# Delta times u plus one: multiplied by VectorE, turned once, copied by ScalarE

## The chip, the cores and the metric

The kernel runs on one core of one Trainium2 chip. The metric is the device time of one launch in microseconds. The kernel before takes 713.55 us (median of 3 runs, 712.55 to 714.0).

## What is computed

A transformer block on 4 sequences of 1024 tokens with 128 channels: a modulated layer norm, a selective state scan as the mixer, a second norm, and a mixture of 8 experts of which each token takes 2. The part that the change touches is the input of the scan:

```python
def _selective_scan(u, A_log, x_proj_w, dt_proj_w, dt_proj_b, D_skip):
    xp = u @ x_proj_w
    delta = jax.nn.softplus(xp[..., :DT_RANK] @ dt_proj_w + dt_proj_b)
    Bm = xp[..., DT_RANK:DT_RANK + N_STATE]
    Cm = xp[..., DT_RANK + N_STATE:]
    A = -jnp.exp(A_log)
    dA = jnp.exp(delta[..., None] * A)
    dBu = delta[..., None] * Bm[:, :, None, :] * u[..., None]
    def step(h, inp):
        dA_t, dBu_t, C_t = inp
        h = dA_t * h + dBu_t
        y = jnp.einsum('bdn,bn->bd', h, C_t)
        return (h, y)
```

u has 256 channels and comes out of a sigmoid. The kernel keeps it as the tanh of half its argument, so that the true value is half of "u plus one"; hence the factor (u + 1) in the code. There are 16 states n.

## The kernel before, in words

The 4096 tokens are cut into 8 segments f of 512 tokens. Channels lie on the 128 partitions, in two halves a. The main loop runs over 128 steps k = 16 s + n: window s works on segment s, step n on state n. In a step, ScalarE makes dA = exp(A delta) for both halves (`decay`, L1013) and scales part of duT, which is delta times (u + 1) with tokens on the partitions, by the token's B (`scale_in`, L1005); GpSimd scales the rest of it (L542). TensorE turns the scaled blocks S back to channels on the partitions (`turn_in`), VectorE scans 512 tokens (`scan`, L1367) into a ring of 6 slots, GpSimd multiplies the ring by C (L559), and TensorE adds it up (`add_state`). Each engine's order is fixed by hand: the instructions stand in program order and every cross-engine dependence is a semaphore.

Everything else is put into "gaps": a step has two, gap 2n and 2n+1, after its first and its second half. `gap_work` calls, in each engine's program, `front` (norm, u, gate of a coming segment), `project` (xproj, delta, B, and duT of the next segment, f = s + 1) and `tail` and `routing` of segments before. Two windows numbered -2 and -1 stand ahead of the loop and hold the gap work of the first segments alone; I call them the prologue. After the last window come 71 expert tiles and 8 sums, the tile stage.

Buffers tie the engines together: S has 3 slots, the banks of turned blocks are 3, dA has 6 slots (3 steps). So ScalarE can be about two steps ahead of VectorE, no more. GpSimd makes its part of S two steps ahead. PSUM banks FA (`front`) and FB (`project`) are each used by one piece after the other, so TensorE waits until the piece before has been read.

In the kernel before, u of each half is turned into FA (gaps 30 and 1, `turns("uT..")`), and VectorE adds one while it copies it to `uT` (L1096, gaps 31 and 2). The later gate product uses FA too and waits for that read. Delta (L1124, gaps 20 and 23) is turned into FB at gaps 24 and 26, and VectorE multiplies it by `uT` into `duT` (L1109, gaps 25 and 27). `scale_in` of the next window's first step, which ScalarE reaches right after gap 27, waits for the second of these.

Of the kernel before, what the change touches and what calls it, by code (L numbers as in the profile page):

```python
# [7 lines left out]
ALU = mybir.AluOpType  # L8
# [4 lines left out]
P = 128  # L13
# [66 lines left out]
def adaln_kernel(nc, xT_d, w1_d, w2_d, wo_d, xproj_d, dtw_d, alog_d, conv_d, cols_d, bo_d, router_d,  # L80
# [5 lines left out]
    with ctx:  # L86
# [63 lines left out]
        gate = sb("gate", [P, 3, HALVES, BANK])  # L150
        uT = sb("uT", [P, CS, MLP])
        duT = sb("duT", [P, 2, CS, MLP])
# [47 lines left out]

        front_all = uT[:, :, :].rearrange("p c m -> p (c m)")
        xs, xsT = tiles_of(front_all, 0, XS_SLOTS, ROW), tiles_of(front_all, (XS_SLOTS + 1) * P, 2)
# [41 lines left out]
        def PO(k):  # L244
            return bank((5, 0)[k % 2])[:, 0:P]

        PIECES = ["raw", "xn", "u0", "u1", "gate0", "gate1", "uT0", "uT1",
                  "xproj", "bt", "dt0", "dt1", "dT0", "dT1",
# [14 lines left out]
        tlog, tseed, tstep, trs_ready = (sem(n) for n in ("tlog", "tseed", "tstep", "trs_ready"))  # L263
        staged = [sem(f"staged{k}") for k in range(2)]
        av_ready, e_ready, lw_ready, w_ready, softplus_step, delta_ready = (
            sem(n) for n in ("av_ready", "e_ready", "lw_ready", "w_ready", "softplus_step", "delta_ready"))
# [319 lines left out]
        def _(pe):  # L586
# [39 lines left out]
            def front(gap, f):  # L626
# [19 lines left out]
                if gap == 0:  # L646
                    product(FB[0:PROJ, :], xproj[:, 1, :], u[:, f % 2, 1, :], False, True).then_inc(filled["xproj"], 1)
                    last_read["FB"] = (read["xproj"], f + 1)
                if gap in (30, 1):
                    a = int(gap == 1)  # L650
                    turns(f"uT{a}", "FA", f + 1, u[:, f % 2, a, :])

            def project(gap, f):
# [12 lines left out]
                if gap in (24, 26):  # L666
                    a = (gap - 24) // 2
                    turns(f"dT{a}", "FB", f + 1, delta[:, f % 2, a, :])

# [217 lines left out]
        def _(act):  # L887
# [39 lines left out]
            def project(gap, f):  # L927
# [10 lines left out]
                if gap in (9, 10):  # L938
                    a = gap - 9
                    act.wait_ge(av_ready, f * HALVES + a + 1)  # L940
                    nc.scalar.activation(ev[:, a, :], ev[:, a, :], ACT.Exp, scale=-1.0).then_inc(e_ready, 1)  # L941
                if gap == 18:
                    act.wait_ge(e_ready, (f + 1) * HALVES)
                    nc.scalar.activation(lw[:, :, :], ev[:, :, :], ACT.Ln, bias=1.0).then_inc(lw_ready, 1)  # L944
# [138 lines left out]
        def _(dve):  # L1083
# [7 lines left out]

            def front(gap, f):
                if gap in (31, 2):
                    a = int(gap == 2)
                    dve.wait_ge(filled[f"uT{a}"], f + 1)
                    V.tensor_scalar(uT[:, :, a * P:(a + 1) * P], FA.rearrange("p (c d) -> p c d", c=CS), 1.0, None, ALU.add  # L1096
                                    ).then_inc(read[f"uT{a}"], 1)

            def project(gap, f):
                if gap in (19, 20, 22, 23):  # L1100
                    softplus((gap - 19) // 3, (gap - 19) % 3, f)
                if gap in (25, 27):
                    a = (gap - 25) // 2
                    dve.wait_ge(filled[f"dT{a}"], f + 1)
                    dve.wait_ge(read[f"uT{a}"], f + 1)
                    if f > 1:
                        dve.wait_ge(scaled_act, act_scaled((f - 1) * NSTATE - 1))
                        dve.wait_ge(scaled_pool, pool_scaled((f - 1) * NSTATE - 1))
                    V.tensor_tensor(duT[:, f % 2, :, a * P:(a + 1) * P], uT[:, :, a * P:(a + 1) * P],  # L1109
                                    FB.rearrange("p (c d) -> p c d", c=CS), ALU.mult).then_inc(read[f"dT{a}"], 1)  # L1110

# [228 lines left out]
            def gap_work(gap, window):  # L1340
# [12 lines left out]
                if inner_ is not None:  # L1353
                    project(gap, inner_)
                if front_ is not None:
                    front(gap, front_)

# [191 lines left out]
```

## Time and profile before

| what | value |
|---|---|
| median of the runs | 713.55 us (712.55 to 714.0) |
| profiled execution | 714.06 us, span 712.3 us |
| PE (TensorE) busy | 622.1 us, 87% |
| DVE (VectorE) busy | 552.2 us, 78% |
| ACT (ScalarE) busy | 545.1 us, 77% |
| POOL (GpSimd) busy | 512.0 us, 72% |
| chain that ended last | PE 43%, ACT 38%, DVE 9%, issue 6%, DMA 2% |

The span is the time from the first to the last instruction of one profiled execution. The shares of busy time are averages over three stages: the prologue to 56 us, the scan windows to about 510 us, and the tile stage, in which TensorE is nearly always busy. The windows of the middle stage are the part to read.

### The profile page before, as it was taken

Reading aid. Unit: us, or ns where it says so; the run is one execution under the profiler, and the core shown is the slowest. Engines: PE = TensorE matmul, PEld = TensorE weight load, DVE = VectorE, ACT = ScalarE, POOL = GpSimd, SP = SyncE. Lnnn points to the kernel's source line nnn. Section 1 sums busy time; section 2 is a strip of 40 time slices with the busy share of each in tenths; the row PEclk is TensorE's granted clock in tenths of the full one; section 3 lists DMA queues with packets and bytes.
Section 4 is the critical chain, followed back from the end, with each engine's and each line's share of the span. In section 5 each row is a group of like instructions: output and inputs, shape, how many; then the busy total and the mean of one; then the engine's idle time right before and its main releaser. Section 6 shows DMA issues by size and latency. Waiting matters only on the chain.

```text
span 712.3 us, 14511 instructions
## 1 busy us (share of the span) xinstructions
PE 622.1 (87%) x4435; PEld 518.5 (73%) x4435; DVE 552.2 (78%) x1170; ACT 545.1 (77%) x1024; POOL 512.0 (72%) x479
## 2 busy tenths in 40 slices
PE   3897789989989988988997997878768999999995
PEld 3444767857767766775775776767667899999994
DVE  4347779899898989989989999889944486555553
ACT  3268989988997997997999799798817656656550
POOL 3147969878899799989989989968915457644441
PEclk9989999999999999999999999979979999999997
DMA  7030436345834554444533563393501122222535
GB/s 232 0 121 2 132 86 163 103 121 159 255 103 111 160 138 107 112 127 125 146 96 107 128 162 103 103 239 119 133 17 51 56 65 84 83 67 63 169 124 186
DMA packets 65196, 82.93 MB, mean 116 GB/s; under 512 B 6960, under 2 KB 55152, under 8 KB 61024
## 3 DMA queue, kind: packets, MB, share of 16 engines
q1 hardware_dynamic: 59648, 70.78, 36.6%
q0 software_dynamic: 4320, 9.12, 3.8%
q10 hardware_dynamic: 1152, 2.10, 0.8%
q8 instruction: 38, 0.62, 0.4%
q14 instruction: 38, 0.31, 0.1%
HBM read 52.19 MB, written 29.78 MB: 115 GB/s over the span
## 4 chain that ended last, share of the span: by engine, by line
PE 43%; ACT 38%; DVE 9%; issue 6%; DMA 2%; POOL 0%; DVEq 0%; ACTq 0%; SPq 0%; POOLq 0%
PE psum L588 28%; PE psum L592 15%; ACT S L1005 14%; ACT dA L1013 13%; DVE ring L1367 4%; ACT xn L909 1%; ACT L1013 1%; ACT L944 1%; DMA ring<-results 1%; ACT soft L937 1%; ACT soft L936 1%; ACT soft L944 1%; ACT hT L891 1%; ACT soft L941 1%; ACT u L914 1%
## 5 line engine op out<-in xcount | busy, mean ns | idle before, releaser
L559 POOL TENSOR_TENSOR ring<-ring,Cb 128x1024 f32<-128x1024 f32 x128 | 279.5, 2185 | 37.0 <-DVE ring L1367 36.4
L592 PEld LDWEIGHTS psum<-ident,S 128*128 128x128 f32 x1024 | 119.4, 143 | 115.0 <-issue 66.8
L592 PE MATMUL psum<-ident,S 128*128 128x128 f32 x1024 | 159.7, 280 | 45.2 <-POOL S L542 12.1
L1013 ACT ACTIVATE dA<-delta,A 128x512 f32<-128x512 f32 x256 | 178.8, 717 | 10.2 <-DVE ring L1367 10.2
L1005 ACT ACTIVATE S<-duT,BT 128x256 f32<-128x256 f32 x384 | 166.6, 502 | 24.5 <-DVE duT L1109 21.2
L592 PE MATMUL psum<-ident,ring 128*128 128x128 f32 x1088 | 159.6, 278 | 4.7 <-DMA ring<-results 4.6
L1367 DVE TENSOR_TENSOR_SCAN ring<-dA,state,psum 128x512 f32<-128x512 f32 x128 | 157.8, 1264 | 1.3 <-PE psum L592 0.6
L1367 DVE TENSOR_TENSOR_SCAN ring<-dA,psum 128x512 f32<-128x512 f32 x128 | 150.4, 1206 | 10.4 <-PE psum L592 10.1
L592 PEld LDWEIGHTS psum<-ident,ring 128*128 128x128 f32 x1088 | 129.5, 144 | 5.8 <-DMA ring<-results 5.2
L580 POOL DMA_INDIRECT results<-xn,result_at x71 | 69.1, 974 | 85.7 <-DVE xn L1496 79.0
L588 PE MATMUL psum<-uT,S 128*128 128x128 f32 x852 | 110.3, 281 | 3.8 <-DVE uT L1478 3.3
L588 PEld LDWEIGHTS psum<-uT,S 128*128 128x128 f32 x852 | 104.3, 197 | 4.8 <-issue 4.8
L1062 ACT COPY S<-gateup_w 128x736 f32 x71 | 57.0, 805 | 51.4 <-PE psum L588 49.9
L542 POOL TENSOR_TENSOR S<-duT,BT 128x256 f32<-128x256 f32 x112 | 75.7, 677 | 5.9 <-DVE duT L1109 5.0
L1501 DVE TENSOR_TENSOR S<-S,psum 128x384 f32<-128x384 f32 x71 | 39.2, 552 | 50.2 <-ACT S L1072 46.5
L472 POOL DMA_INDIRECT token_rows<-h2r,pos x64 | 65.0, 1016 | 17.8 <-issue 9.6
L588 PE MATMUL psum<-hT,w1c 128*128 128x512 f32 x128 | 67.6, 629 | 2.1 <-ACT hT L891 2.1
L588 PE MATMUL psum<-soft,S 128*128 (+1 forms) x426 | 59.5, 276 | 2.0 <-DVE S L1501 1.9
L588 PEld LDWEIGHTS psum<-soft,S 128*128 128x128 f32 (+1 forms) x426 | 53.2, 192 | 2.8 <-issue 2.8
L1072 ACT ACTIVATE S<-psum 128x384 f32<-128x384 f32 x71 | 34.8, 490 | 25.0 <-PE psum L588 24.3
L508 POOL TENSOR_SCALAR xT<-xT,gabo 128x1024 f32<-128x1024 f32 x4 | 11.5, 2870 | 33.5 <-PE psum L592 25.0
L1478 DVE COPY uT<-psum 128x128 f32<-128x128 f32 x71 | 20.5, 289 | 13.9 <-PE psum L592 13.7
(226 smaller groups left out, 745.1 us busy)
## 6 DMA issues: line engine op xcount, KB each, us to landing
Cb<-c_rows SPq DMA_DIRECT2D x32, 1024.0 KB, 6.0
token_rows<-zeros SPq DMA_DIRECT2D x64, 272.0 KB, 7.1
uT<-token_rows SPq DMA_DIRECT2D x71, 68.0 KB, 1.8
ring<-results SPq DMA_DIRECT2D x8, 512.0 KB, 5.0
xT<-in_xT SPq DMA_DIRECT2D x4, 512.0 KB, 5.1
out_T<-xT ACTq DMA_DIRECT2D x8, 256.0 KB, 2.3
stage<-in_xT SPq DMA_DIRECT2D x6, 256.0 KB, 7.3
gateup_w<-in_gate SPq DMA_DIRECT2D x1, 1408.0 KB, 10.2
```

What stands on the lines that cost most here:

```text
L472: nc.gpsimd.indirect_dma_start(token_rows, bass.IndirectOffsetOnAxis(ap=pos[:, j, g * CS + c:g * CS + c + 1], axis=0), h2r[:, j, g * CS + ...
L542: nc.gpsimd.tensor_tensor(S[:, k % S_SLOTS, CS - own:, :], duT[:, s % 2, CS - own:, :], BT[:, s % 2, CS - own:, n:n + 1].to_broadcast([P, ...
L559: nc.gpsimd.tensor_tensor(ring[:, k % RING, :, 0:BANK], ring[:, k % RING, :, 1:], Cb[:, group_ % 2, own, :].unsqueeze(1).to_broadcast([P, ...
L580: nc.gpsimd.indirect_dma_start(results, bass.IndirectOffsetOnAxis(ap=result_at[:, t % (2 * XS_SLOTS):t % (2 * XS_SLOTS) + 1], axis=0), ob[ ...
L588: return nc.tensor.matmul(out, lhsT, rhs, start=start, stop=stop)
L592: return nc.tensor.matmul(out, block_in, ident[at, at], is_transpose=True, start=start, stop=True, skip_group_check=True)
L1005: nc.scalar.activation(S[:, k % S_SLOTS, c, :], duT[:, s % 2, c, :], ACT.Identity, scale=BT[:, s % 2, c, n:n + 1]).then_inc(scaled_act, 1)
L1013: nc.scalar.activation(dA[:, (k * HALVES + a) % DA_SLOTS, :], delta[:, s % 2, a, :], ACT.Exp, scale=A[:, a, n:n + 1]).then_inc(da_ready, 1)
L1062: nc.scalar.copy(both_w[:, par % 2, :], gateup_w[:, ds(e * 2 * INTER, INTER + NIN * P)]).then_inc(weights_copied, 1)
L1072: nc.scalar.activation(silu[:, par % 2, :], PG(par)[:, 0:NIN * P], ACT.Silu).then_inc(silu_ready, 1)
L1367: V.tensor_tensor_scan(ring[:, k % RING, a, 1:], dA[:, (k * HALVES + a) % DA_SLOTS, :], db(k, a), state[:, n, a:a + 1] if s % SEG else 0.0 ...
L1501: V.tensor_tensor(innerT[:, par % 2, :], silu[:, par % 2, :], PU(par)[:, 0:NIN * P], ALU.mult).then_inc(inner_ready, 1)
```

## The change

The sum and the product change places. VectorE multiplies (u + 1) by delta with channels on the partitions into a new buffer `du` in one instruction per half, after delta (gaps 21 and 24). TensorE turns `du` in the places in which it turned delta (gaps 24 and 26). ScalarE copies the turned block from FB to `duT` (gaps 25 and 27). The turning of u, its copy and the multiplication of turned blocks are gone. `du` takes the memory of `uT`. Both tensors that the new product reads lie in SBUF; each of the removed instructions read one from PSUM.

```diff
@@ tensor engine
-                if gap in (30, 1):
-                    a = int(gap == 1)
-                    turns(f"uT{a}", "FA", f + 1, u[:, f % 2, a, :])
@@
                 if gap in (24, 26):
                     a = (gap - 24) // 2
-                    turns(f"dT{a}", "FB", f + 1, delta[:, f % 2, a, :])
+                    pe.wait_ge(du_ready, HALVES * f + a + 1)
+                    turns(f"dT{a}", "FB", f + 1, du[:, a, :])
@@ scalar engine
+                if gap in (25, 27):
+                    a = (gap - 25) // 2
+                    act.wait_ge(filled[f"dT{a}"], f + 1)
+                    if f > 1:
+                        act.wait_ge(scaled_pool, pool_scaled((f - 1) * NSTATE - 1))
+                    nc.scalar.copy(duT[:, f % 2, :, a * P:(a + 1) * P], FB.rearrange("p (c d) -> p c d", c=CS)
+                                   ).then_inc(read[f"dT{a}"], 1)
@@ vector engine
-            def front(gap, f):
-                if gap in (31, 2):
-                    a = int(gap == 2)
-                    dve.wait_ge(filled[f"uT{a}"], f + 1)
-                    V.tensor_scalar(uT[:, :, a * P:(a + 1) * P], FA.rearrange("p (c d) -> p c d", c=CS), 1.0, None, ALU.add
-                                    ).then_inc(read[f"uT{a}"], 1)
@@
-                if gap in (25, 27):
-                    a = (gap - 25) // 2
-                    dve.wait_ge(filled[f"dT{a}"], f + 1)
-                    dve.wait_ge(read[f"uT{a}"], f + 1)
-                    if f > 1:
-                        dve.wait_ge(scaled_act, act_scaled((f - 1) * NSTATE - 1))
-                        dve.wait_ge(scaled_pool, pool_scaled((f - 1) * NSTATE - 1))
-                    V.tensor_tensor(duT[:, f % 2, :, a * P:(a + 1) * P], uT[:, :, a * P:(a + 1) * P],
-                                    FB.rearrange("p (c d) -> p c d", c=CS), ALU.mult).then_inc(read[f"dT{a}"], 1)
+                if gap in (21, 24):
+                    a = (gap - 21) // 3
+                    dve.wait_ge(delta_ready, HALVES * f + a + 1)
+                    dve.wait_ge(read[f"u{a}"], f + 1)
+                    wait(dve, filled[f"dT{a}"], f)
+                    V.scalar_tensor_tensor(du[:, a, :], u[:, f % 2, a, :], 1.0, delta[:, f % 2, a, :], ALU.add, ALU.mult
+                                           ).then_inc(du_ready, 1)
```

VectorE, window 2 from the second scan of step 10 to the scans of step 12 and on, in the kernel before (L1117 to L1124 make delta, L1089 is the norm before the router, the scans are L1367):

```order
L1367 SCALAR_TENSOR_TENSOR ring<-dA,psum 128x512 x2
L1117 SCALAR_TENSOR_TENSOR soft<-psum,soft 128x512
L1118 SCALAR_TENSOR_TENSOR psum<-psum,soft 128x512
L1367 SCALAR_TENSOR_TENSOR ring<-dA,psum 128x512
L1089 TENSOR_SCALAR xn<-psum,tstat,trs 128x128 x4
L1121 TENSOR_TENSOR psum<-soft,psum 128x512
L1124 TENSOR_TENSOR delta<-soft,psum 128x512
L1367 SCALAR_TENSOR_TENSOR ring<-dA,psum 128x512 x2
L1109 TENSOR_TENSOR duT<-uT,psum 128x4x128
L1367 SCALAR_TENSOR_TENSOR ring<-dA,psum 128x512 x2
L1109 TENSOR_TENSOR duT<-uT,psum 128x4x128
```

The same place in the changed kernel (its lines: scan L1362, delta L1114 to L1121, norm L1095, the new product L1106):

```order
L1362 SCALAR_TENSOR_TENSOR ring<-dA,psum 128x512
L1106 SCALAR_TENSOR_TENSOR du<-u,delta 128x512
L1362 SCALAR_TENSOR_TENSOR ring<-dA,psum 128x512
L1114 SCALAR_TENSOR_TENSOR soft<-psum,soft 128x512
L1115 SCALAR_TENSOR_TENSOR psum<-psum,soft 128x512
L1362 SCALAR_TENSOR_TENSOR ring<-dA,psum 128x512
L1095 TENSOR_SCALAR xn<-psum,tstat,trs 128x128 x4
L1118 TENSOR_TENSOR psum<-soft,psum 128x512
L1121 TENSOR_TENSOR delta<-soft,psum 128x512
L1362 SCALAR_TENSOR_TENSOR ring<-dA,psum 128x512
L1106 SCALAR_TENSOR_TENSOR du<-u,delta 128x512
L1362 SCALAR_TENSOR_TENSOR ring<-dA,psum 128x512 x6
```

The two products moved ahead: the first now stands before the first scan of step 11, the second between the two scans of step 12, and no gap work stands between the scans of steps 12 to 14.

ScalarE, the same stage of window 2, before (L1005 is the scaling, L1013 the decay, L891 the second norm's modulation):

```order
L1013 ACTIVATE dA<-delta,A 128x512 x2
L1005 ACTIVATE S<-duT,BT 128x256 x3
L1013 ACTIVATE dA<-delta,A 128x512
L891 ACTIVATE hT<-psum,mod 128x512
L1013 ACTIVATE dA<-delta,A 128x512
L1005 ACTIVATE S<-duT,BT 128x256 x3
L1013 ACTIVATE dA<-delta,A 128x512
```

And after (scaling L1011, decay L1019, modulation L890, the new copy L946):

```order
L1019 ACTIVATE dA<-delta,A 128x512 x2
L946 COPY duT<-psum 128x4x128
L1011 ACTIVATE S<-duT,BT 128x256 x3
L1019 ACTIVATE dA<-delta,A 128x512
L890 ACTIVATE hT<-psum,mod 128x512
L1019 ACTIVATE dA<-delta,A 128x512
L946 COPY duT<-psum 128x4x128
L1011 ACTIVATE S<-duT,BT 128x256 x3
```

The first copy stands ahead of the scaling for step 15, the second ahead of the scaling for the next window's first step.

## Rows read from the trace of the kernel before

**Rows 1.** Busy time by engine in one scan window; columns: stretch, length, busy (instructions):

```profile
200.57:259.53 58.96, 53.41 (x375) 42.27 (x374) 53.99 (x82) 54.63 (x109) 53.55 (x50) 1.00 0.48 125
```

**Rows 2.** Waits by engine and line; columns: total us, times, longest:

```profile
ACT S L1005 <- DVE duT L1109: 21.2, 7, 3.7
```

**Rows 3.** Chain of waits, 200 to 260 us; columns: start, length, what:

```profile
214.26 1.94 PE psum L592 x16
...
225.32 0.20 DVE stat L1164
```

**Rows 4.** Groups of instructions by line; columns: count, busy us, mean ns, idle before:

```profile
L1096 DVE TENSOR_SCALAR uT<-psum 128x512 f32<-128x512 f32 x16 | 10.9, 683 | 5.3 <-PE psum L592 5.1
L1109 DVE TENSOR_TENSOR duT<-uT,psum 128x512 f32<-128x512 f32 x16 | 10.8, 675 | 5.6 <-PE psum L592 5.4
L1117 DVE SCALAR_TENSOR_TENSOR soft<-psum,soft 128x512 f32<-128x512 f32 x16 | 10.8, 674 | 5.5 <-ACT soft L944 4.7 <-ACT psum L949 0.8
L914 ACT ACTIVATE u<-psum,zhalf 128x512 f32<-128x512 f32 x16 | 10.8, 678 | 12.3 <-PE psum L621 9.5 <-PE psum L588 2.7
L1437 DVE TENSOR_TENSOR w1c<-ring 128x1024 f32<-128x1024 f32 x1 | 2.0, 1974 | 0.0
```

**Rows 5.** Timeline of window 2's end and window 3's start; columns: start, length, what [idle before]:

```profile
220.91 1.31 ACT L1005 ACTIVATE S<-duT,BT 128x256 f32<-128x256 f32 x3 [3.72 <-DVE duT L1109]
...
226.78 0.66 DVE L1096 TENSOR_SCALAR uT<-psum 128x512 f32<-128x512 f32 x1
...
232.27 0.69 DVE L1096 TENSOR_SCALAR uT<-psum 128x512 f32<-128x512 f32 x1
...
245.51 2.20 POOL L559 TENSOR_TENSOR ring<-ring,Cb 128x1024 f32<-128x1024 f32 x1 [0.63 <-DVE ring L1367]
```

**Rows 6.** Timeline of window 3, steps 10 to 15, three engines:

```profile
266.01 2.44 DVE L1367 TENSOR_TENSOR_SCAN ring<-dA,state,psum 128x512 f32<-128x512 f32 x2
267.15 0.22 POOL L492 TENSOR_SCALAR trs<-tstat 128x4 f32<-128x4 f32 x1
269.16 0.63 PE L592 MATMUL psum<-ident,S 128*128 128x128 f32 x4 [1.74 <-POOL S L542]
273.05 2.19 POOL L559 TENSOR_TENSOR ring<-ring,Cb 128x1024 f32<-128x1024 f32 x1
273.32 2.44 DVE L1367 TENSOR_TENSOR_SCAN ring<-dA,state,psum 128x512 f32<-128x512 f32 x2
275.19 0.61 POOL L542 TENSOR_TENSOR S<-duT,BT 128x256 f32<-128x256 f32 x1
277.58 0.60 PE L592 MATMUL psum<-ident,S 128*128 128x128 f32 x4
279.22 0.62 POOL L542 TENSOR_TENSOR S<-duT,BT 128x256 f32<-128x256 f32 x1
281.06 0.60 PE L592 MATMUL psum<-ident,S 128*128 128x128 f32 x4
```

**Rows 7.** Timeline of VectorE beside GpSimd where the tile stage starts:

```profile
514.52 4.30 POOL L559 TENSOR_TENSOR ring<-ring,Cb 128x1024 f32<-128x1024 f32 x2
...
518.01 0.84 DVE L1484 TENSOR_TENSOR result_at<-uT,aside 128x1 int32<-128x1 f32 x1
```

**Rows 8.** The line L1484 by itself; columns: duration ns min/median/max:

```profile
L1484 DVE TENSOR_TENSOR result_at<-uT,aside x71: 146/149/843, 518.0 to 690.0; 128x1 int32<-128x1 f32 x71
```

**Rows 9.** Timeline of the prologue:

```profile
32.32 1.88 PE L588 MATMUL psum<-u,xproj 128*96 128x512 f32 x4
35.42 1.13 PE L588 MATMUL psum<-hT,w 128*128 128x512 f32 x2 [0.78 <-DVE uT L1096]
56.03 1.31 ACT L1005 ACTIVATE S<-duT,BT 128x256 f32<-128x256 f32 x3 [1.97 <-DVE duT L1109]
```

**Rows 10.** Timeline of window 0, end:

```profile
92.72 0.69 DVE L1117 SCALAR_TENSOR_TENSOR soft<-psum,soft 128x512 f32<-128x512 f32 x1 [4.11 <-ACT soft L944]
108.03 1.31 ACT L1005 ACTIVATE S<-duT,BT 128x256 f32<-128x256 f32 x3 [2.73 <-DVE duT L1109]
```

More of the change, by code:

```diff
@@ L150, in adaln_kernel @@
         gate = sb("gate", [P, 3, HALVES, BANK])
-        uT = sb("uT", [P, CS, MLP])
+        du = sb("du", [P, HALVES, BANK])
         duT = sb("duT", [P, 2, CS, MLP])
@@ L199, in tiles_of @@
             return area[:, at:at + count * width].rearrange("p (k h) -> p k h", k=count)
-        front_all = uT[:, :, :].rearrange("p c m -> p (c m)")
+        front_all = du[:, :, :].rearrange("p a t -> p (a t)")
         xs, xsT = tiles_of(front_all, 0, XS_SLOTS, ROW), tiles_of(front_all, (XS_SLOTS + 1) * P, 2)
@@ L245, in PO @@
             return bank((5, 0)[k % 2])[:, 0:P]
-        PIECES = ["raw", "xn", "u0", "u1", "gate0", "gate1", "uT0", "uT1",
+        PIECES = ["raw", "xn", "u0", "u1", "gate0", "gate1",
                   "xproj", "bt", "dt0", "dt1", "dT0", "dT1",
@@ L264, in adaln_kernel @@
         staged = [sem(f"staged{k}") for k in range(2)]
+        du_ready = sem("du_ready")
         av_ready, e_ready, lw_ready, w_ready, softplus_step, delta_ready = (
@@ L1354, in gap_work @@
                     project(gap, inner_)
-                if front_ is not None:
-                    front(gap, front_)
             def scan(k, a):
```

## The prediction

> **What bounds the kernel now.** I read the table of stretches first, then the waits, the chain, and at last the timelines of single windows, engine beside engine. A full window takes 58.96 us, and in it four engines are busy 53.4, 54.0, 54.6 and 53.6 us [rows 1]: no engine is the bound alone, and each has only some 5 us to spare. ScalarE's longest wait is for the multiplication into duT: 21.2 us in 7 waits, one at each window's end, 3.7 us at most [rows 2]. That looks like the prize of this change, and I think that it is not. The question is what holds the window while ScalarE waits.
>
> Going through one period: TensorE takes up work at 214.26 and is on the chain until VectorE gets the router's logits at 225.32 [rows 3]. The next window shows who had released it: TensorE waits 1.74 us at 269.16 for GpSimd's part of S [rows 6]; at 214.26 I take it for the same. Further ahead, at 245.51, GpSimd itself waited for VectorE's scan [rows 5]. So a period is: VectorE from the logits (225.3) to the scan that GpSimd waits for (245.5), some 20 us; GpSimd from there to its S just ahead of the product at 273.05 [rows 6], 28 us; TensorE for the rest of the 58.96, some 11 us, to the next logits. ScalarE is ahead of all this by its two steps of buffers, and its 3.7 us are slack.
>
> **The change part by part.** The sum is made against the profiled execution (714.06 us, span 712.3); I carry the difference over to the median, 713.55.
>
> 1. Removed in the VectorE part of the period. The two additions of one cost 0.683 us each [rows 4], and both lie at 226.78 and 232.27, in the 20 us where VectorE paces [rows 5]. I count 0.6 of each, since the records of neighbours overlap a little: 1.2 us a boundary. Five boundaries have them beside the routing work (segments 3 to 7): -6.0 us if all else follows.
>
> 2. Removed on TensorE: 16 groups of four turns of u, 0.60 us each by the record of a like group (277.58 [rows 6]), and a wait of the gate product for VectorE. In the windows they lie behind the logits, where VectorE paces, and I give them nothing.
>
> 3. ScalarE's copies, 16. The nearest row is its reading of a 128x512 bank, 0.678 us [rows 4], some 0.57 behind another. Both stand between the scaling for step 14 and that for the next window's first step, where ScalarE waits 3.72 us now [rows 5]. The first makes it wait in its own queue for the first turned half; behind it stand the scaling of step 15 and two decays, each needed some microseconds later by scans that are not yet due. The second can start when the second turned half is there, which is where VectorE's multiplication started before, and takes the same time. So the handoff gains nothing but about 0.1 us, and the copies cost nothing while the 3.7 us are there. Without that cover they would cost 2 x 0.57 = 1.15 us a window.
>
> 4. VectorE's new products, 16. Duration between 0.674, the like instruction with one tensor in PSUM, and 0.99, half of the one large instruction that reads SBUF alone, which took 1.974 for twice the elements [rows 4]. I take 0.68; that one had a strided operand. They take the place of multiplications of 0.675, so VectorE's work in this part is as before, but it stands before the second scan of step 12, which TensorE needs: that scan ends at 275.7, and TensorE's turn of step 14's S comes at 277.58 [rows 6], a slack of 1.8 us, of which 1.2 go for the two products.
>
> 5. What the new products meet. The L1484 at 518.01, which reads two SBUF tensors, took 0.84 us where the median of its 71 is 0.149 [rows 8]; it ended at 518.85, and GpSimd's products ended at 518.82 [rows 7]. All the other instructions of VectorE in the scan windows have an operand in PSUM and run beside GpSimd without loss. So a new product may have to wait for GpSimd's present instruction: between 0 and 2.19 us (the ring product at 273.05 [rows 6]), 16 times; and GpSimd may have to wait for it in turn, 0 to 0.68 us. The page "SBUF — State Buffer" of the Trainium skill (section "SBUF: two separate sides") says just that: a VectorE instruction with two SBUF inputs and a GpSimd instruction that reads SBUF exclude each other for the whole instruction, whichever starts first; by that rule, the trace agrees for the one direction that it shows.
>
> The phase decides the size. The first product comes after the second scan of step 10, at about 267.2, where GpSimd has small instructions of 0.2 us (267.15) [rows 6]: VectorE gets in at once, and GpSimd, which paces here, is put back by up to 0.6. The second comes after step 12's first scan, at about 274.5; GpSimd's ring product runs from 273.05 to 275.2 and its S from 275.19 to 275.8 [rows 6]. With GpSimd 0.6 earlier than now, VectorE meets the end of the one or the whole of the other: 0.1 to 0.7 us. If it waits for the S as well, the scan is late, GpSimd's S for step 15 (279.22) is late, and TensorE, which takes it at 281.06 [rows 6], loses what was left. So of 1.2 us gained a boundary, 0.6 goes to the first product and 0 to 0.6 to the second: I take -0.3 a boundary, 5 x -0.3 = -1.5 us.
>
> 6. Windows 0 and 1 have no routing, and are paced by ScalarE's logarithm, then VectorE from 92.72 to the duT at 108.03, then ScalarE again [rows 10]. The products (+1.2) and the turn of step 14 with the copy behind it come in place of two multiplications; with what the second product waits for S I get between -0.2 and +0.5 for each: +0.3 for both.
>
> 7. The prologue. The xproj product starts a turn (0.5) earlier, and the gate product, which started at 35.42, follows it at its end, 34.20 [rows 9]: -1.7. At the other end the tanh of the next segment, done in the wait before 56.03 till now, comes behind the copies: +0.5. So -1.2.
>
> The tile stage is as it was. Sum: -1.5 + 0.3 - 1.2 = **-2.4 us**, 711.7 for the profiled execution, 711.2 for the median.
>
> **The rivals.**
> - Only the prologue gains, the windows give nothing: 713.55 - 1.2 = 712.4. For it: half of point 5's range. Chance 0.15.
> - No mutual waiting of note: point 1 in full, the additions gone and nothing lost, 5 x -1.2, with -1.7 from the prologue: 705.9. Against it: rows 7. Chance 0.16.
> - Slower, by VectorE caught behind whole ring products. Place: the second product before step 12's second scan, and the first one in windows 0 and 1, where GpSimd waits for the same scan. Price: 2.2 us for a product caught, less the slack of 1.8 - 1.2 = 0.6; with the first product's 0.6 on GpSimd and -1.2 from point 1 some +1.0 a window for five, +1.5 for each of the first two, -1.2 for the prologue: +6.8, 720.3. It decides from about 1.2 us of waiting a window on. Chance 0.14.
> - Slower, by ScalarE becoming the bound: then 7 x 1.15 less the prologue's gain, +6.9: 720.4. Against it: it would be busy 54.6 + 1.15 = 55.8 of 58.9. Chance 0.05.
> - The wait of rows 2 was the real limit: 21.2 less 14 copies of 0.57, less the prologue: 713.55 - 13.2 - 1.2 = 699.1. Against it: rows 3 and 6, where TensorE and GpSimd work without a pause while ScalarE waits. Chance 0.05.
>
> **How the numbers follow.** My forecast has 0.45, its own range 708.5 to 714. A run can tell 0.2% from no change, 1.4 us. Faster by more: 0.36 of my 0.45, 0.16 and 0.05, with a little of the first rival, 0.58. Within: 0.20. Slower: 0.14 + 0.05 and 0.03 from mine, 0.22. The range 705.5 to 717 leaves out the last rival and half of the two slow ones.
>
> **What the profile after would show.** Right: products on VectorE with a mean above 0.68 us and some of 0.8 to 1.3; the small GpSimd instructions or the S beside them late; ScalarE's wait at the window's end for the turned half instead of duT, still 1 to 3 us; windows of 58.3 to 58.9 us; the first S at about 54.8. Wrong: products of 2 us and more (then slower), products all at 0.68 and windows near 57.7 (then the second rival), or a ScalarE without waits.

## The result, and the profile after

The changed kernel takes 715.78 us (median; 713.81 to 718.69), the kernel before on the same chip 714.01 (711.94 to 715.58): ratio 1.0024, 95% interval 1.0014 to 1.0034. The forecast was 711.2; the time moved the other way, by 1.8 us. The profiled span is 714.2 us for 712.3.

The stretches of two windows in the changed kernel (columns as in [rows 1]):

```profile
201.38:261.28 59.90, 53.40 (x374) 42.05 (x375) 54.86 (x83) 55.75 (x111) 55.22 (x50) 1.00 0.47 127
261.28:320.77 59.49, 51.72 (x361) 40.42 (x360) 53.29 (x82) 55.64 (x111) 53.82 (x50) 1.00 0.45 123
```

The window that took 58.96 us [rows 1] takes 59.90. ScalarE has its copies more (55.75 for 54.63 us). GpSimd is busy 1.7 us longer with the same 50 instructions: something holds them. The waits of ScalarE and GpSimd in the whole changed kernel (total us, times, longest):

```profile
ACT duT L946 <- PE psum L593: 23.8, 15, 4.2
POOL ring L560 <- DVE ring L1362: 37.1, 33, 5.5
```

ScalarE's wait of [rows 2] is gone by name and is back before its copies, as large as it was (23.8 for 21.2 us): that fits slack, and e4 below shows that it is. GpSimd's wait for scans is hardly larger in sum than before (37.1 for 36.4 us), but it has moved, as the timelines show. The groups that answer to [rows 4] (count, busy us, mean ns, idle before):

```profile
L1106 DVE SCALAR_TENSOR_TENSOR du<-u,delta 128x512 f32<-128x512 f32 x16 | 13.9, 867 | 0.1
L1114 DVE SCALAR_TENSOR_TENSOR soft<-psum,soft 128x512 f32<-128x512 f32 x16 | 10.8, 678 | 6.8 <-ACT soft L950 6.6
L946 ACT COPY duT<-psum 128x512 f32<-128x512 f32 x16 | 9.4, 586 | 23.8 <-PE psum L593 23.8
```

The product has a mean of 0.867 us; its like with one operand in PSUM keeps 0.678. Which of them are long shows in the timeline of window 3, steps 10 to 15, the place of [rows 6]:

```profile
267.06 0.20 POOL L497 TENSOR_TENSOR trs<-trs 128x4 f32<-128x4 f32 x1
267.26 0.67 DVE L1106 SCALAR_TENSOR_TENSOR du<-u,delta 128x512 f32<-128x512 f32 x1
267.34 0.64 POOL L499 TENSOR_SCALAR trs<-trs 128x4 f32<-128x4 f32 x1
...
273.99 1.27 DVE L1362 TENSOR_TENSOR_SCAN ring<-dA,state,psum 128x512 f32<-128x512 f32 x1
274.97 0.61 POOL L543 TENSOR_TENSOR S<-duT,BT 128x256 f32<-128x256 f32 x1
275.18 0.95 DVE L1106 SCALAR_TENSOR_TENSOR du<-u,delta 128x512 f32<-128x512 f32 x1
276.06 5.96 DVE L1362 TENSOR_TENSOR_SCAN ring<-dA,state,psum 128x512 f32<-128x512 f32 x5
277.41 2.19 POOL L560 TENSOR_TENSOR ring<-ring,Cb 128x1024 f32<-128x1024 f32 x1 [1.83 <-DVE ring L1362]
280.79 0.62 POOL L543 TENSOR_TENSOR S<-duT,BT 128x256 f32<-128x256 f32 x1
281.51 0.63 PE L593 MATMUL psum<-ident,S 128*128 128x128 f32 x4 [0.36 <-issue]
```

The first product gets in at once and GpSimd's 0.20 us instruction takes 0.64. The second runs into GpSimd's S and takes 0.95, ending 0.55 after that S. Then comes a wait that the prediction did not have: GpSimd, its S done, waits 1.83 us for the second scan of step 12, which stands behind the second product. In the kernel before the same place reads

```profile
275.84 2.19 POOL L559 TENSOR_TENSOR ring<-ring,Cb 128x1024 f32<-128x1024 f32 x1
```

without a wait: that scan ended at 275.76 [rows 6], 0.08 us ahead. Where GpSimd did wait, in the changed kernel, it starts 0.08 us after the scan too, so there was no slack at all. By window, from 0 to 6, GpSimd started 0.08, 0.08, 0.78, 0.08, 0.70, 0.08 and 1.44 us after this scan in the kernel before, and 0.08 in each in the changed one. In windows 2 to 6 the second product took 1.43, 0.95, 1.27, 0.95 and 1.90 us; in windows 0 and 1, and as the first product everywhere, 0.66 to 0.69. The long ones of windows 2, 4 and 6 met the tail of a ring product and not only an S. In window 2:

```profile
213.67 2.18 POOL L560 TENSOR_TENSOR ring<-ring,Cb 128x1024 f32<-128x1024 f32 x1
214.99 1.43 DVE L1106 SCALAR_TENSOR_TENSOR du<-u,delta 128x512 f32<-128x512 f32 x1
215.82 1.06 POOL L543 TENSOR_TENSOR S<-duT,BT 128x256 f32<-128x256 f32 x1
217.62 2.19 POOL L560 TENSOR_TENSOR ring<-ring,Cb 128x1024 f32<-128x1024 f32 x1 [0.74 <-DVE ring L1362]
```

The product ends at 216.41, 0.56 after the ring product's end, GpSimd's S has 1.06 us instead of 0.61, and GpSimd waits 0.74 for the scan. So windows 2 and 4 show a wait of 0.74 and a held S, windows 3 and 5 a wait of 1.83.

For the prologue, [rows 9]: the first scaling starts 1.28 us earlier.

```profile
54.75 1.30 ACT L1011 ACTIVATE S<-duT,BT 128x256 f32<-128x256 f32 x3
```

What follows is measured by one mark a window, VectorE's first reading of the router's logits, whose start the trace gives to 0.01 us. There are eight marks, in windows 1 to 7 and one in the tile stage; the four periods from window 1's to window 5's are compared, in one profiled execution of each kernel. Before it stands at 166.30 (window 1) and at 401.43 (window 5): four windows take 235.13 us. After: 165.87 and 403.46, 237.59 us, +0.62 a window. The same stretch of every other kernel (e15 and e16 repeat two of them, and show how far one profile is to be trusted: e15 differs from after by 0.30 a window, almost all of it in one period, e16 from e5 by 0.01):

| kernel | four windows | a window, against before | median us | ratio (95%) |
|---|---|---|---|---|
| before | 235.13 | | 713.5 to 714.4 | 1 |
| after | 237.59 | +0.62 | 715.78 | 1.0024 (1.0014 to 1.0034) |
| after again (e15) | 238.82 | +0.92 | 715.19 | 1.0020 (1.0005 to 1.0034) |
| products behind delta (e1) | 240.84 | +1.43 | 721.85 | 1.0106 (1.0089 to 1.0124) |
| the same, PSUM operand (e2) | 236.62 | +0.37 | 717.64 | 1.0049 (1.0033 to 1.0065) |
| without u (e3) | 232.04 | -0.77 | 708.59 | 0.9928 (0.9910 to 0.9945) |
| before with ScalarE's copies (e4) | 235.11 | 0.00 | 714.46 | 1.0008 (0.9993 to 1.0022) |
| after, PSUM operand (e5) | 235.62 | +0.12 | 714.21 | 1.0010 (0.9998 to 1.0022) |
| the same again (e16) | 235.56 | +0.11 | 713.07 | 0.9988 (0.9973 to 1.0002) |
| after without products (e6) | 231.89 | -0.81 | 706.25 | 0.9911 (0.9888 to 0.9934) |
| copies by VectorE (e7) | 238.16 | +0.76 | 716.58 | 1.0055 (1.0034 to 1.0076) |
| u plus one by ScalarE (e8) | 234.98 | -0.04 | 715.38 | 1.0030 (1.0017 to 1.0044) |
| first product alone (e9) | 234.01 | -0.28 | 710.01 | 0.9933 (0.9913 to 0.9953) |
| second product alone (e10) | 235.47 | +0.09 | 712.26 | 0.9968 (0.9957 to 0.9979) |
| additions at gaps 9 and 11 (e11) | 237.78 | +0.66 | 716.35 | 1.0042 (1.0024 to 1.0059) |
| products at gaps 24 and 26 (e12) | 241.10 | +1.49 | 722.55 | 1.0123 (1.0101 to 1.0145) |
| lock-free behind the scan (e13) | 231.90 | -0.81 | 708.29 | 0.9913 (0.9893 to 0.9932) |
| segment 0 alone (e14) | 235.12 | 0.00 | 710.16 | 0.9944 (0.9924 to 0.9965) |

The median has a second part that the windows do not explain. In the session of e15, nine executions of the changed kernel had a mean granted clock of 0.957 to 0.967 and took 713.9 to 718.3 us, three had 0.974 to 0.976 and took 713.9 to 715.3; the kernel before had 0.970 to 0.978 and took 711.7 to 715.8. Why the changed kernel has the lower clock more often, and how much of the 1.8 us goes with it, was not tested. The arguments below therefore rest on the marks first.

### The profile page after: what moved, and what is told of

The parts are those of the page before. It is cut to its first block and busy times, and to the rows that moved or that the text cites. A ratio compares the mean times of both kernels' runs of the same rounds, so it can differ in the third digit from the quotient of the medians.

```text
span 714.2 us, 14394 instructions
## 1 busy us (share of the span) xinstructions
PE 613.6 (86%) x4371; PEld 510.1 (71%) x4371; DVE 548.0 (77%) x1154; ACT 554.2 (78%) x1040; POOL 516.6 (72%) x479
## 5 line engine op out<-in xcount | busy, mean ns | idle before, releaser
L560 POOL TENSOR_TENSOR ring<-ring,Cb 128x1024 f32<-128x1024 f32 x128 | 280.4, 2192 | 37.6 <-DVE ring L1362 37.1
L1019 ACT ACTIVATE dA<-delta,A 128x512 f32<-128x512 f32 x256 | 178.5, 715 | 4.9 <-DVE ring L1362 4.7
L1011 ACT ACTIVATE S<-duT,BT 128x256 f32<-128x256 f32 x384 | 166.6, 502 | 0.6
L1362 DVE TENSOR_TENSOR_SCAN ring<-dA,psum 128x512 f32<-128x512 f32 x128 | 150.7, 1207 | 17.1 <-PE psum L593 15.5
L1362 DVE TENSOR_TENSOR_SCAN ring<-dA,state,psum 128x512 f32<-128x512 f32 x128 | 158.4, 1267 | 4.4 <-PE psum L593 2.8
L589 PE MATMUL psum<-du,S 128*128 128x128 f32 x852 | 110.9, 282 | 3.8 <-DVE du L1473 3.3
L589 PEld LDWEIGHTS psum<-du,S 128*128 128x128 f32 x852 | 104.5, 198 | 4.8 <-issue 4.8
L543 POOL TENSOR_TENSOR S<-duT,BT 128x256 f32<-128x256 f32 x112 | 77.3, 691 | 6.1 <-ACT duT L946 5.1
L589 PE MATMUL psum<-hT,w1c 128*128 128x512 f32 x128 | 66.1, 616 | 2.1 <-ACT hT L890 2.1
L593 PE MATMUL psum<-ident,du 128*128 128x128 f32 x135 | 30.0, 282 | 6.0 <-DVE delta L1121 3.5
```

The lines of the kernel that those rows point to most:

```text
L543: nc.gpsimd.tensor_tensor(S[:, k % S_SLOTS, CS - own:, :], duT[:, s % 2, CS - own:, :], BT[:, s % 2, CS - own:, n:n + 1].to_broadcast([P, ...
L560: nc.gpsimd.tensor_tensor(ring[:, k % RING, :, 0:BANK], ring[:, k % RING, :, 1:], Cb[:, group_ % 2, own, :].unsqueeze(1).to_broadcast([P, ...
L589: return nc.tensor.matmul(out, lhsT, rhs, start=start, stop=stop)
L593: return nc.tensor.matmul(out, block_in, ident[at, at], is_transpose=True, start=start, stop=True, skip_group_check=True)
L1011: nc.scalar.activation(S[:, k % S_SLOTS, c, :], duT[:, s % 2, c, :], ACT.Identity, scale=BT[:, s % 2, c, n:n + 1]).then_inc(scaled_act, 1)
L1019: nc.scalar.activation(dA[:, (k * HALVES + a) % DA_SLOTS, :], delta[:, s % 2, a, :], ACT.Exp, scale=A[:, a, n:n + 1]).then_inc(da_ready, 1)
```

## The experiments

Theory A: VectorE's product with two SBUF inputs and GpSimd shut each other out, and the windows lose by it. Theory B: ScalarE's two copies make the windows longer.

**e1 and e2: the exclusion by itself.** Both put the products directly behind delta; they differ in one operand. Both also have TensorE's first turn wait for both products, and ScalarE's next write to FB for the first, so the pair is clean between its two kernels and not against the kernel before.

```diff
-                if gap in (21, 24):
+                if gap in (20, 23):
...
-  V.scalar_tensor_tensor(du[:, a, :], u[:, f % 2, a, :], 1.0, delta[:, f % 2, a, :], ALU.add, ALU.mult)
+  V.scalar_tensor_tensor(du[:, a, :], u[:, f % 2, a, :], 1.0, FB, ALU.add, ALU.mult)      # e2 only
```

> The changed kernel with each product of VectorE standing directly behind the delta that it multiplies (gaps 20 and 23 instead of 21 and 24); ScalarE's next write to FB waits for the first product, TensorE's first turn for both. The pair to the next kernel, which differs only in where the second operand lies. Theory A (VectorE's product with two SBUF inputs and GpSimd shut each other out, and the windows lose by it): products of 0.67 to 2 us, mean over 0.75; time 712 to 718 us, and 2 to 5 us above the next kernel. Theory B (the windows are longer because ScalarE now has two copies more): as long as the next kernel, within 1 us.

> As the kernel before it, but the product reads FB (in PSUM) in place of delta, so its value lacks the masked logarithm: one SBUF and one PSUM input, same order, same count. Theory A: all 16 products at 0.67 to 0.70 us, GpSimd's small instructions at 0.2, time 709 to 713 us. Theory B: same time as its pair within 1 us, near 715.

The product's group in e1, then in e2:

```profile
L1106 DVE SCALAR_TENSOR_TENSOR du<-u,delta 128x512 f32<-128x512 f32 x16 | 16.8, 1050 | 0.6
```

```profile
L1106 DVE SCALAR_TENSOR_TENSOR du<-u,psum 128x512 f32<-128x512 f32 x16 | 11.0, 687 | 0.6
```

4.2 us between the pair, 1.06 a window: the exclusion is real and costs, and Theory B, which had them alike, falls here. But both came out 4 to 5 us above what Theory A expected of them. Without any exclusion e2 is still slower than before. So something beside the exclusion costs, the place of the products or those waits (TensorE waits 1.1 us for the products in each of windows 2 to 5 of e1, 0.8 to 0.9 in two of them in e2).

**e3: the removal alone.**

```diff
-  if gap in (30, 1): turns(f"uT{a}", "FA", f + 1, u[:, f % 2, a, :])
-  V.tensor_scalar(uT[...], FA..., 1.0, None, ALU.add)
-  V.tensor_tensor(duT[...], uT[...], FB..., ALU.mult)
+  V.tensor_scalar(duT[...], FB..., 1.5, None, ALU.mult)
```

> The kernel before without the turns of u and the additions of one (TensorE's and VectorE's), and with the multiplication by the turned u replaced by one by a constant (so u is left out of duT): what the removal alone brings. By the prediction's points 1 and 7: 7 to 8 us less than before, 706. By the trace of the changed kernel, where the stage of 20 us behind the logits got only 0.3 us shorter instead of 1.2: 1 to 3 us less, 711 to 713, of which 1.2 in the prologue.

708.6 us lies between the two ranges: 5.5 us less, 0.77 a window for the 1.2 of the prediction. Why not 1.2 shows behind the logits in e6, which has the same removal. TensorE, let through earlier by VectorE, waits 1.16 us for the S of step 66 (window 4, step 2):

```profile
282.73 1.30 ACT L1010 ACTIVATE S<-duT,BT 128x256 f32<-128x256 f32 x3
286.68 0.62 POOL L543 TENSOR_TENSOR S<-duT,BT 128x256 f32<-128x256 f32 x1
287.40 0.63 PE L593 MATMUL psum<-ident,S 128*128 128x128 f32 x4 [1.16 <-ACT S L1010]
```

The profile puts this wait down to ScalarE, but the rows counted by step say otherwise: ScalarE's part of that S was done at 284.03, GpSimd's at 287.30, 0.10 us before TensorE starts. In the kernel before the same turn, at 290.59, waited 0.40 us, again until 0.10 after GpSimd's part. So it is with all 80 waits of over 0.3 us for an S between window 1's mark and window 5's in before, after, e3 and e6: they end 0.10 us after GpSimd's part and 2.9 us or more after ScalarE's. GpSimd is the one that TensorE waits for, and the page's chain, which gives ScalarE 38% in the kernel before, goes wrong at such places.

In the kernel before, GpSimd waits for scans only in the first third of these periods. Behind window 2's, in the kernel before, it waits 0.81, 1.39 and 0.63 us; in e6 the first of these is gone, the others are 1.38 and 0.63. The place of the first, before and then in e6:

```profile
237.99 2.19 POOL L559 TENSOR_TENSOR ring<-ring,Cb 128x1024 f32<-128x1024 f32 x1 [0.81 <-DVE ring L1367]
```

```profile
234.68 2.17 POOL L560 TENSOR_TENSOR ring<-ring,Cb 128x1024 f32<-128x1024 f32 x1
```

That is 12.67 us after the mark (225.32) and 11.84 after it (222.84): 0.83 us gained, as much as GpSimd had waited there and not the whole of VectorE's 1.2.

**e4: ScalarE's copies alone.**

```diff
+                if gap in (25, 27):
+                    act.wait_ge(filled[f"dT{a}"], f + 1)
+                    nc.scalar.copy(ev[:, a, :], delta[:, f % 2, a, :])
```

> The kernel before with ScalarE's two extra copies of 128x512 a window in the places of the changed kernel (gaps 25 and 27, each waiting for the turned half as there), from delta to a free buffer; nothing else changed. Theory A: 0 to 1 us slower than before, 714 to 715. Theory B: 3 to 6 us slower, 717 to 720, with ScalarE's wait at the window's end gone and its scaling late for TensorE.

1.0008, and 0.00 us a window: the copies cost nothing, as the prediction had it. In its profile the period from window 5's mark to window 6's is 60.02 us for 57.76, outside the four that are compared; its median does not show that, and the cause stays open.

**e5: the changed kernel with a PSUM operand, every place kept.**

```diff
+                    k, half = (f - 1) * NSTATE + 11 + a, a
+                    dve.wait_ge(turned_in, k * HALVES + half + 1)
-  ... delta[:, f % 2, a, :], ALU.add, ALU.mult)
+  ... db(k, half), ALU.add, ALU.mult)
```

> The changed kernel, every instruction in its place, but the product of segments 1 to 7 reads in place of delta the PSUM bank that the next scan reads (after the same wait as that scan), so du has a wrong second factor: one SBUF and one PSUM input at the places of the change. What the mutual exclusion costs there. From the pair that was run (4.2 us with the products behind delta): all 14 products at 0.67 to 0.69 us, 711 to 713.5 us. If not the exclusion but the two places lose the time: 714.5 to 716.

All 14 at 0.66 us (mean 661 ns), but 714.2 us, above the 711 to 713.5 of the exclusion as the sole cause and just below the 714.5 to 716 of the places alone; per window 0.49 us less than after. Both take part. And with no exclusion left, GpSimd still waits for that scan:

```profile
274.23 0.62 POOL L543 TENSOR_TENSOR S<-duT,BT 128x256 f32<-128x256 f32 x1
274.89 0.66 DVE L1111 SCALAR_TENSOR_TENSOR du<-u,psum 128x512 f32<-128x512 f32 x1
...
275.47 5.96 DVE L1367 TENSOR_TENSOR_SCAN ring<-dA,state,psum 128x512 f32<-128x512 f32 x5
276.83 2.19 POOL L560 TENSOR_TENSOR ring<-ring,Cb 128x1024 f32<-128x1024 f32 x1 [1.98 <-DVE ring L1367]
```

This made the third theory: the product costs by its place, ahead of a scan that GpSimd takes up with no slack.

**e6 and e7: no products; copies by VectorE.**

```diff
-                    V.scalar_tensor_tensor(du[:, a, :], ...)                        # e6
-                    turns(f"dT{a}", "FB", f + 1, du[:, a, :])
+                    turns(f"dT{a}", "FB", f + 1, delta[:, f % 2, a, :])
...
-                    nc.scalar.copy(duT[...], FB...)                                 # e7
+                    V.tensor_copy(duT[...], FB...)
```

> The changed kernel without VectorE's products: TensorE turns delta as before, ScalarE copies it (u is left out of duT). If the products (0.67 us each, the waiting included) are what ate the gain of the removed additions: 706 to 708.5 us, near the kernel before without u. If ScalarE's copies ahead of its scaling ate it: 713 to 716.

> The changed kernel with the two copies a window made by VectorE in the places of the old multiplications (gaps 25 and 27) instead of ScalarE. If ScalarE's copies cost nothing, 1.35 us more on VectorE a window, of which half to all shows: 719 to 723 us. If ScalarE was the one that the change overloaded: 711 to 714.

Without products the whole gain of the removal is there: 0.9911, 0.81 a window. GpSimd's place reads

```profile
271.83 0.60 POOL L543 TENSOR_TENSOR S<-duT,BT 128x256 f32<-128x256 f32 x1
272.66 2.19 POOL L560 TENSOR_TENSOR ring<-ring,Cb 128x1024 f32<-128x1024 f32 x1 [0.23 <-DVE ring L1354]
```

0.23 us of waiting instead of 1.8 to 2.0. From e6 to e5 is the price of the lock-free products where the change has them: (235.62 - 231.89) / 4 = 0.93 us a window, for 1.32 us of work. TensorE's turns of du are not what costs: in windows 2 to 5 of e5 and of after it has no wait of over 0.4 us for a product. e3 (VectorE multiplies at gaps 25 and 27) and e6 (ScalarE copies there) have the same windows, to 0.04 us: behind the scan, VectorE's 1.35 us were free. e7 missed its expectation of 719 to 723: its copies at gaps 25 and 27 cost 0.14 a window against after, which is less than after and e15 differ, and 0.3% in the median, since that place is nearly free.

**e8: the removal by another way.**

```diff
-  turns of u at gaps 30 and 1, V.tensor_scalar(uT[...], FA..., 1.0, None, ALU.add) at gaps 31 and 2
+  turns of u at gaps 29 and 31, nc.scalar.activation(uT[...], FA..., ACT.Identity, bias=1.0) at gaps 31 and 1
```

> The kernel before, its multiplication of turned blocks kept, but u plus one copied out of FA by ScalarE (gaps 31 and 1) instead of VectorE (31 and 2), with TensorE's turns of u at gaps 29 and 31 instead of 30 and 1. It removes the same 16 VectorE instructions from the same stage as the change, adds as much to ScalarE, and brings no product with two SBUF inputs. If the removal is worth what the kernel without u showed (5.5 us) and ScalarE's work is nearly free (0.4 us for two copies a window): 708.5 to 711 us. If ScalarE's work behind the logits, or TensorE's turns in other places, cost more: 712 to 715.

The second case, and a little past it: nothing gained in the windows, 0.3% slower in all. Its edit does two things, ScalarE's added work and TensorE's turns in other places, and which of them eats the 0.77 us was not separated.

**e9 and e10: one product each.**

```diff
-                if gap in (21, 24):
+                if gap == 21:      # e9; e10: gap == 24
```

> The changed kernel with its first product alone (gap 21); the second half of delta is turned and copied without u. Without products it took 706.3 us, with both 715.8. Theory (the products stand ahead of step 12's second scan, for which GpSimd waits, so that each one's time shows there, and the second also meets GpSimd's S): the first costs 0.45 to 0.7 us a window and little in the prologue: 709 to 711.5 us, the smaller part. Rival (the loss is a matter of the second product and its mutual exclusion alone): 706 to 708 us.

> The changed kernel with its second product alone (gap 24); the first half of delta is turned and copied without u. Theory: 710.5 to 713 us, the larger part, its durations 0.67 to 1.5 us. Rival (the two places count alike and the exclusion is shared): the same as with the first alone within 1 us, near 711.

As the theory of the place had it, against e6: the first costs (234.01 - 231.89) / 4 = 0.53 us a window, the second (235.47 - 231.89) / 4 = 0.89, together 1.42, and with both (after) it is (237.59 - 231.89) / 4 = 1.42. GpSimd's ring product of step 12 in e9, then in e10:

```profile
274.51 2.18 POOL L560 TENSOR_TENSOR ring<-ring,Cb 128x1024 f32<-128x1024 f32 x1 [0.37 <-DVE ring L1363]
```

```profile
274.22 2.20 POOL L560 TENSOR_TENSOR ring<-ring,Cb 128x1024 f32<-128x1024 f32 x1 [1.82 <-DVE ring L1363]
```

The first product has VectorE and GpSimd late together; the second makes GpSimd wait. These rows are of window 3. By the profile of e15 instead of after, both together are 1.73 a window, so that the sum agrees to 0.3 us and no better.

**e11 and e12: other places.**

```diff
-  turns of u at gaps 30 and 1, additions at 31 and 2, raw rows turned at gap 10      # e11
+  turns of u at gaps 8 and 10, additions at 9 and 11, raw rows turned at gap 12
...
-  products at gaps 21 and 24, turns of du at 24 and 26, copies at 25 and 27          # e12
+  products at gaps 24 and 26, turns of du at 25 and 27, copies at 26 and 27
```

> The kernel before with the same turns of u and the same additions of one on VectorE, but moved out of the stretch behind the logits: turned at gaps 8 and 10 (the first window at 8 and 9), added at 9 and 11; TensorE's turn of the raw rows goes from gap 10 to 12. If VectorE's time is dear only behind the logits, where it paces, and about free from the scans of steps 4 and 5 on: 708.5 to 711 us. If it is as dear there (GpSimd waits for those scans), or TensorE's new waits for VectorE in FA cost what is gained: 713 to 716 us.

> The changed kernel with its products moved behind the place that was found dear: at gaps 24 and 26 instead of 21 and 24, turned at gaps 25 and 27, copied at 26 and 27. The first now stands where the second did, the second behind the first scan of step 13. If time ahead of step 12's second scan is dear and time behind it free: 0.7 us a window less ahead of it, 710.5 to 713 us, below the changed kernel. If the later handoff of duT makes ScalarE's scaling for the next window's first step late (it had 1.9 to 2.5 us of slack at the first copy), or the second product is held by GpSimd again: 714 to 719 us.

Both came out above even the slower of their two ranges, e11 by 0.4 us and e12 by 3.6. In e11 each window is 0.66 us longer than before, and VectorE's wait for ScalarE's logarithm is 11.4 us in sum for 4.7 before; whether the scans behind the additions or TensorE's turn of u in FA is to blame was not separated. e12 shows the exclusion at its dearest. Its second product starts 1.0 us into a ring product for whose scan GpSimd had waited, and has to sit out the rest:

```profile
281.67 2.19 POOL L560 TENSOR_TENSOR ring<-ring,Cb 128x1024 f32<-128x1024 f32 x1 [0.80 <-DVE ring L1362]
282.69 1.72 DVE L1106 SCALAR_TENSOR_TENSOR du<-u,delta 128x512 f32<-128x512 f32 x1
284.33 1.27 DVE L1362 TENSOR_TENSOR_SCAN ring<-dA,state,psum 128x512 f32<-128x512 f32 x1
```

It ends at 284.41, 0.55 us after the ring product's end at 283.86, and takes 1.71 to 1.79 us in all seven windows. This is the mechanism of the prediction's slow rival. The change as made meets only the tails of ring products, in windows 2, 4 and 6.

**e13 to e16.**

```diff
+                if gap in (25, 27) and f > 0:                                      # e13, on e6
+                    V.scalar_tensor_tensor(du[:, a, :], u[:, f % 2, a, :], 1.0, db(k, 0), ALU.add, ALU.mult)
...
+  the changed code where f == 0, the code before where f > 0                       # e14, on before
```

> The changed kernel without its products (TensorE turns delta, u is left out), with two lock-free products a window whose result nobody uses, at gaps 25 and 27 of windows 0 to 6: one SBUF and one PSUM operand (the bank of the next scan), behind step 12's second scan instead of ahead of it. Without any product it took 706.3 us, with lock-free ones at gaps 21 and 24 714.2. If the place is what costs: 706 to 707.5 us, and GpSimd does not wait for step 12's second scan. If VectorE's time costs anywhere: 710 to 714 us.

> The kernel before, with the change applied to segment 0 alone, whose duT is made in the prologue; segments 1 to 7 as before. The first scaling comes 1.3 us earlier, as in the changed kernel, and no window is touched. If that lead is kept: 712.2 to 713.2 us with before at 714.0, ratio 0.997 to 0.999. If windows 0 and 1 take it back (they are paced by other things): 713.5 to 714.5.

> The changed kernel itself, as the pair of the next one: 715 to 716 us.

> The changed kernel with the PSUM operand in the products of segments 1 to 7 (du has a wrong second factor). The trace of the first run puts its logits 2.0 us earlier than the changed kernel's over four windows: 1.5 to 3 us below its pair. If the exclusion costs nothing in the sum: the same time.

e13 has in the windows as much work on VectorE as e5, behind the scan instead of ahead of it, and takes what e6 without any takes: the same four windows (231.90 for 231.89 us) and the same ratio (0.9913 for 0.9911; its median, 708.3, is 0.8 us above the range expected and 2.0 above e6's, and that of before beside it is 0.8 higher too). So VectorE's time is free behind that scan and dear ahead of it. Its two products and GpSimd:

```profile
272.71 0.66 DVE L1102 SCALAR_TENSOR_TENSOR du<-u,psum 128x512 f32<-128x512 f32 x1
272.87 2.19 POOL L560 TENSOR_TENSOR ring<-ring,Cb 128x1024 f32<-128x1024 f32 x1 [0.29 <-DVE ring L1359]
273.29 2.45 DVE L1359 TENSOR_TENSOR_SCAN ring<-dA,state,psum 128x512 f32<-128x512 f32 x2
```

e15 and e16, on one chip, are 2.1 us apart (0.82 us a window), where after and e5, not run side by side, had 0.49 a window. The exclusion in the change costs 0.5 to 0.8 us a window.

e14 is faster than both kernels: 0.9944, 710.2 for 714.3 us. That is more than the 1 to 2 us expected. The windows are as before; the logits stand 0.68 us earlier in windows 1 to 6, and 1.16 in window 7. Most of the lead of the first scaling (55.13 for 56.03) is kept. The rest is the tile stage, 195.7 us for 199.5 from window 7's logits to the end of the span. Two stretches of it in the kernel before, then in e14 (columns as in [rows 1]; the granted clock is third from the end):

```profile
530.00:540.00 10.00, 9.36 (x60) 8.11 (x59) 4.19 (x16) 3.08 (x5) 2.10 (x3) 0.86 0.08 22
550.00:560.00 10.00, 7.78 (x55) 7.40 (x54) 5.40 (x20) 4.86 (x9) 5.39 (x10) 0.83 0.19 56
```

```profile
530.00:540.00 10.00, 9.36 (x71) 8.11 (x71) 5.34 (x19) 4.16 (x7) 3.25 (x4) 0.98 0.13 36
550.00:560.00 10.00, 8.62 (x79) 8.44 (x78) 5.36 (x21) 5.70 (x9) 5.28 (x7) 1.00 0.20 56
```

If TensorE set the pace throughout, the clock would account for 10 x 0.12 + 10 x 0.17 = 2.9 of the 3.8 us; it was busy 7.8 to 9.4 of each 10 us, so this estimate is an upper one. Why a lead of 1 us turns into that was not tested; the executions of before at a like mean clock (0.975 to 0.978) still took 711.7 us and more, those of e14 708.0 to 710.7 at 0.976. So the change in the prologue is worth some 0.7 to 1.2 us by the marks of the windows, and what the tile stage adds stays open.

## Why the prediction was wrong

By its own points, with what a window measured:

- **What bounds the kernel.** Right: ScalarE's 21.2 us were slack (e4: copies free), and the period runs through VectorE, GpSimd and TensorE. The profile puts the wait before 214.26 down to ScalarE (1.23 us), but GpSimd's part of that S ended at 214.16 and ScalarE's at 209.38, so taking it for GpSimd's was right.
- **Point 1, the additions: -1.2 a window.** Right in kind, too large: -0.77 (e3). GpSimd had waited 0.81 us for the first scan that came earlier, and then sets the pace itself.
- **Point 3, the copies: 0.** Right: 0.00 (e4).
- **Point 4, the products' work: 0. This is the step that failed.** It read "they take the place of multiplications of 0.675, so VectorE's work in this part is as before", and allowed the second scan of step 12 a slack of 1.8 us, measured to TensorE's turn at 277.58. The removed multiplications stood behind that scan, where time was free (e3 against e6, 0.04; e13 against e6, 0.00). The products stand ahead of it. And TensorE was the wrong one to measure to: GpSimd multiplies the scan's output at 275.84, 0.08 us after the scan's end, which is no slack (0.7 us in windows 2 and 4). The price is +0.93 a window (e5 against e6), more than the removal brings.
- **Point 5, the exclusion: +0.6 and 0 to 0.6, as +0.9.** Right in kind, in both directions and for both phases (the first product gets in and puts GpSimd back 0.44, the second meets GpSimd's S). Its size was 0.5 to 0.8. The second product met the end of a ring product in windows 2, 4 and 6 (0.8, 0.6 and 1.2 us above its 0.67) and an S in windows 3 and 5 (0.3), the two cases that the point names with 0.1 to 0.7. The page "SBUF — State Buffer" of the Trainium skill (section "SBUF: two separate sides") has the pair exclusive for the whole instruction, whoever starts first; the runs agree for both: 1.72 us of a product behind a ring product, 0.64 for a GpSimd instruction of 0.20.
- **Point 6, windows 0 and 1: +0.3.** Too small: of the 1.28 us with which they start, 0.43 is left at window 1's logits, +0.85.
- **Point 7, the prologue: -1.2.** Right: -1.28.

The sum with the measured terms: -0.77 + 0.93 + 0.49 = +0.65 a window, for +0.62 in the trace of after. This is no independent check: the terms are differences along one row of kernels (before, e3; e6, e5; e5, after), and all that the agreement says is that e3 and e6 are alike to 0.04. Over the profile: -1.28 + 0.85 + 4 x 0.62, then +1.04 in the next period and -0.20 in the last, is +2.9 at window 7's logits, and +1.9 at the end of the span. The slow rival had the right sign with another mechanism: products caught in every window are those of e12, and in the change only window 6's 1.2 us comes near its price of 2.2. No rival was "the place ahead of the scan costs more than the additions bring".

## What to carry to other kernels

An instruction that moves past another has its price set by everyone who waits for what now stands behind it. List all readers of each result that is delayed and take the smallest slack, not that of the reader that one has in mind; a reader that starts without a recorded wait may have no slack (0.08 us after the scan here, the same as when it had waited). The name that a profile gives to a wait for several semaphores is to be tested by the ends of all of them, step by step. Where two engines can exclude each other, ask what the other has just been released by: a two-SBUF product that comes 1 us behind a scan that GpSimd waited for sits out the rest of GpSimd's product in every window (e12). And a change whose gain lies in one place can be applied there alone (e14).

## What was not expected of the hardware

- An instruction of VectorE with two SBUF inputs takes 0.66 to 0.69 us when it gets in first, as with a PSUM operand, and when it is caught it ends 0.55 us after GpSimd's instruction: it loses the remainder of that instruction, less 0.1 us (275.58 to 276.13 in the changed kernel, 283.86 to 284.41 in e12).
- GpSimd's own recorded time grows while it is held (0.20 to 0.64 us), so an engine that shows more busy time with the same count of instructions may be one that waits.
- The tile stage's granted clock differed (0.83 to 1.00 in one stretch of 10 us) between kernels whose tile stage has the same code and starts 1 us apart. No run shows why.
